# Two attention blocks with split queries: stacked halves for the scores, aggregated moments, and another order of slots

## The reference, cut to what matters

```
x = x + attention(ln(x), ctx, mask)    # X: 16 heads of 32, keys masked
x = x + ternary_ffn(quantised ln(x))   # one 512 x 512 product, rows quantised to 8 bits
x = x + attention(ln(x), ctx)          # Y: 16 heads of 64, with an output projection
x = x + ffn(ln(x))                     # Z: FFT, sparse product, inverse FFT, real part; folded into one matrix m
```

## Time and profile before

| | |
|---|---|
| median of 3 runs | 1170.33 us (1170.12 to 1173.37) |
| the profiled execution | 1169.09 us, its span 1167.3 us |
| PE busy | 957.4 us, 82% |
| DVE busy | 898.2 us, 77% |
| ACT busy | 634.9 us, 54% |
| POOL busy | 492.7 us, 42% |
| granted TensorE clock, mean | 0.91 |
| DMA moved | 131.95 MB, 113 GB/s |
| period of an item in the steady part | 110 us |

### The profile page before, as it was taken

The page is one execution under the profiler, slowest core; times in us unless marked ns, Lnnn a source line. Parts: engine busy times, 40 slices in busy tenths (PEclk is TensorE's granted clock), DMA queues, the critical chain, the costliest instruction groups (busy, mean ns, idle before and its releaser), DMA issues.

```text
span 1167.3 us, 17877 instructions
## 1 busy us (share of the span) xinstructions
PE 957.4 (82%) x6211; PEld 508.7 (44%) x6227; DVE 898.2 (77%) x1704; ACT 634.9 (54%) x1748; POOL 492.7 (42%) x437
## 2 busy tenths in 40 slices
PE   1896994693777997898799889979997898599694
PEld 0443463352343554454454445544554455344341
DVE  8777379537989799979987998899789978835732
ACT  2333174233577658657763776477558656614701
POOL 0224024111646267337723762475267336802603
PEclk9988997895699998999899989989998999699797
DMA  9623025543846747585648656746856483551612
GB/s 368 195 86 108 1 67 137 121 116 74 144 88 105 134 84 128 96 167 110 116 102 146 100 107 122 147 89 120 141 110 123 90 143 69 111 103 25 118 39 72
DMA packets 379026, 131.95 MB, mean 113 GB/s; under 512 B 365148, under 2 KB 370812, under 8 KB 375609
## 3 DMA queue, kind: packets, MB, share of 16 engines
q1 hardware_dynamic: 378937, 130.82, 54.7%
HBM read 35.14 MB, written 15.96 MB: 44 GB/s over the span
## 4 chain that ended last, share of the span: by engine, by line
DVE 35%; PE 24%; DMA 10%; ACT 9%; POOL 8%; SPq 8%; issue 7%; ACTq 0%; POOLq 0%; DVEq 0%
PE wb L170 6%; PE wb L171 6%; PE wb L172 6%; DMA prT<-ph 6%; DVE ph L1180 4%; ACT pr L770 3%; DVE mx L1158 3%; SPq L494 3%; PE wb L1307 2%; DVE xr L1112 2%; DVE stats L1052 2%; POOL xr L666 2%; DVE xn L1083 2%; DVE parts L862 2%; ACT xn L800 2%
## 5 line engine op out<-in xcount | busy, mean ns | idle before, releaser
L644 POOL TENSOR_TENSOR pr<-pr,sm 128x616 f32<-128x616 f32 x128 | 166.1, 1298 | 289.9 <-DVE sm L1175 283.0
L770 ACT ACTIVATE pr<-scores,mx,factor 128x77 f32<-128x77 f32 x576 | 229.6, 425 | 21.6 <-DVE mx L1161 18.4
L170 PE MATMUL wb<-xT,wq_hl 128*128 128x512 f16 x384 | 150.8, 393 | 9.6 <-DVE qc L1105 4.2
L171 PE MATMUL wb<-xT,wq_hl 128*128 128x512 f16 x384 | 150.6, 392 | 0.0
L172 PE MATMUL wb<-xT,wq_hl 128*128 128x512 f16 x384 | 149.6, 390 | 0.0
L783 ACT ACTIVATE ph<-pr 128x618 f16<-128x618 f32 x128 | 93.5, 732 | 97.0 <-DMA prT<-ph 75.6
L635 POOL TENSOR_TENSOR rstd<-var,mhalf 128x2 f32<-128x2 f32 (+1 forms) x48 | 51.2, 1067 | 221.4 <-DVE var L1068 221.4
L770 ACT ACTIVATION_READ_ACCUMULATOR pr<-scores,mx,factor 128x1 f32 x576 | 123.9, 215 | 0.0
L1112 DVE SCALAR_TENSOR_TENSOR xr<-wb,factor,xr 128x512 f32<-128x512 f32 x72 | 53.3, 740 | 71.7 <-PE wb L172 71.7
L1158 DVE TENSOR_REDUCE mx<-scores 128x8 f32<-128x616 f32 x128 | 101.1, 790 | 5.7 <-PE scores L172 5.6
L170 PE MATMUL scores<-k1b,qc 128*128 128x154 f16 x256 | 61.0, 256 | 49.3 <-DVE qc L1105 29.1
(11 more groups left out here) (218 smaller groups left out, 2502.6 us busy)
## 6 DMA issues: line engine op xcount, KB each, us to landing
xr<-in_x SPq DMA_DIRECT2D x6, 1024.0 KB, 6.1
out_x<-xr SPq DMA_DIRECT2D x6, 1024.0 KB, 5.2
prT<-in_dft SPq DMA_DIRECT2D x1, 3072.0 KB, 22.2
k1b<-scr_k SPq DMA_DIRECT2D x16, 154.0 KB, 6.8
scr_v<-k1b SPq DMA_DIRECT2D x9, 256.0 KB, 3.2
scr_k<-k1b SPq DMA_DIRECT2D x7, 308.0 KB, 3.1
xr<-in_wf SPq DMA_DIRECT2D x2, 1024.0 KB, 10.6
x<-in_x SPq DMA_DIRECT2D x2, 1024.0 KB, 10.7
```

The lines of the kernel that those rows point to most:

```text
L170: pe.matmul(out, lhs(0), rhs(0), start=start, stop=False, **kw)
L171: pe.matmul(out, lhs(0), rhs(1), start=False, stop=False, **kw)
L644: pool.tensor_tensor(v, v, s, ALU.mult).then_inc(probs_ready, 1)
L770: ins = act.activation(pr[U % 3][:, h // 4, cols], sc[:, U % 2, h // 4, cols], ACT.Exp, bias=mx[:, U % 4, h:h + 1], scale=k["factor"][:, f ...
```

## The change

1. **Stacked queries.** Each head pair's queries stand as one stack of 128 partitions: the 64 high rows in the lower half, their 64 low rows in the upper (`qc` and `q0T`, index 0 for the first two heads or first head, 1 for the other). K stands twice, once in either half (`load_k` issues each piece twice). A score is then two products, one with K's high and one with its low half, and contains low x low too. For X a group is the mask row and 4 matmuls of 154 columns, for Y 8 matmuls of 77 columns. ACT's and DVE's drains write where the halves already fit; what must cross partitions is moved by three DMAs of 64 x 512 per projection (`move_upper` once the high half is drained, `move_low` twice once the low half is). PE waits for these DMAs (`q0_stacked`, `q1_stacked`) where it waited for the drains. The low halves of Y's queries pass through `q0T`, so X's projections wait for their moves.
2. **Moments.** `ln_group` is one `bn_aggr` per tile; POOL adds the epsilon and negates the mean in two small operations more.
3. **Mask row.** It is kept in DRAM and loaded by SP; ACT's copy goes. The clear of `k1b` goes.
4. **Order.** New `FILLS` and `UNITS` (X in slots 0 to 4 and 6 to 8, nothing in 5 and 9), `HEADWISE` of 11 units in place of 9, `LOW_BY_POOL` of 2 in place of 6, other slots in `APPLY`, `LOWER`, `BIAS`; ACT and DVE take a unit's probabilities before the drains, not after.

```diff
-FILLS = [[("Z", "f", 0)],
-         [("Z", "f", 1)],
...
+FILLS = [[("Z", "f", 0), ("Z", "f", 1)],
+         [("Z", "f", 2), ("Z", "f", 3)],
+         [("Y", "pv", 4), ("Y", "pv", 5), ("Y", "pv", 6), ("Y", "pv", 7)],
          [],
+         [],
+         [("Z", "out", 0), ("Z", "out", 1), ("Z", "out", 2), ("X", "pv", 0)],
+         [("X", "pv", 1)],
+         [("Z", "out", 3), ("Y", "q", 0), ("Y", "q", 1)],
+         [("Y", "q", 2), ("Y", "q", 3)],
+         [("Y", "q", 4), ("Y", "q", 5)],
...
-HEADWISE = {("X", 0), ("X", 2), ("X", 5), ("X", 7), ("Y", 1), ("Y", 2), ("Y", 3), ("Y", 5), ("Y", 7)}
+HEADWISE = {("X", 0), ("X", 2), ("X", 5), ("X", 6), ("X", 7), ("Y", 1), ("Y", 2), ("Y", 3), ("Y", 4), ("Y", 6), ("Y", 7)}
-LOW_BY_POOL = {("X", 4), ("X", 6), ("X", 7), ("Y", 1), ("Y", 2), ("Y", 3)}
+LOW_BY_POOL = {("X", 7), ("Y", 1)}
...
                 for j in range(n):
                     rows = slice(j * w, (j + 1) * w)
-                    sp.dma_start(kb[rows, :, :, j, :].rearrange("p h m n -> p (h m) n"),
-                                 scr_k[rows, :, b * KEYS:(b + 1) * KEYS]).then_inc(kl, 16)
+                    for copy in range(2):
+                        r0 = copy * H1 + j * w % H1
+                        sp.dma_start(kb[r0:r0 + w, :, :, j, :].rearrange("p h m n -> p (h m) n"),
+                                     scr_k[rows, :, b * KEYS:(b + 1) * KEYS]).then_inc(kl, 16)
...
+            def move_upper(use):
...
+                sp.wait_ge(bank_hi, HIGH[use] + 1)
+                sp.dma_start(stack[0:H1, 1, m, :], stack[H1:P, 0, m, :]).then_inc(uppers_moved, 16)
+            def move_low(use, last):
+                stack, low, stacked = stack_of(use)
+                sp.wait_ge(bank_free, FILL[use] + 1)
+                sp.dma_start(stack[H1:P, 1, use[2], :], low[H1:P, :]).then_inc(stacked, 16)
+                sp.wait_ge(uppers_moved, 16 * (UPPER[last] + 1))
+                sp.dma_start(stack[H1:P, 0, use[2], :], low[0:H1, :]).then_inc(stacked, 16)
...
+                projected = [use for use in SLOT_DRAINS[g] if use[1] == "q"]
+                for use in projected:
+                    move_upper(use)
                 if unit_at(g - 2):
                     turn(*unit_at(g - 2))
+                for use in projected:
+                    move_low(use, projected[-1])
...
-                dve.tensor_tensor(m, e, o, ALU.add)
-                dve.tensor_tensor(h, e, o, ALU.subtract)
...
+                for t in range(t0, t0 + width):
+                    ins = dve.bn_aggr(moments[:, j, t, :], stats[:, j, t, :])
+                ins.then_inc(ln_var, 1)
...
-                if stage == "X" and u < 2:
-                    pe.wait_ge(bank_free, FILL["W", "q", 2 * u + 1, b] + 1)
+                if stage == "X" and u < 2:
+                    for m in (2 * u, 2 * u + 1):
+                        pe.wait_ge(q0_stacked[m], 32 * (b + 1))
...
+                        for e in range(4):
+                            for h in range(2):
+                                ins = pe.matmul(sc[:, U % 2, gg, e * KEYS:(e + 1) * KEYS], qc[:, e % 2, 2 * g + e // 2, tok],
+                                                k1b[:, h, 2 * g + e // 2, e % 2, :],
+                                                start=e == 0 and h == 0, stop=h == 1, skip_group_check=True)
```

154 lines of the change are left out of this document (79 added, 75 removed).

## The result

The changed kernel takes **1280.45 us** (median of four runs, 1278.3 to 1282.46), the kernel before 1171.01 us in the same comparison. The ratio is **1.092, 95% interval 1.090 to 1.095**: 109 us slower. The forecast was 1210 us with a range up to 1250. The sign is right, the size is not.

A forecast was written before the change was run, and what follows sets the result against it. DVE sets the pace in the item's first part, PE by a small margin in the second. Items of 104.6 + 5.7 + 6.4 + 2.6 = 119.3 us gave 49 more, less 9, on 1169.1: 1210 us, range 1132 to 1250.

The forecast's parts named there:

- Scores: PE's score matmuls in X and Y units: the new shapes save 3.9 us of PE per item.
- short matmuls cost as much: Rival, chance 0.02: short score matmuls cost as much as those of 154 columns, PE saves nothing there, 1225 us.
- Mean and variance: DVE's statistics groups: aggregations replace seven small operations, saving 0.5 us a group, 3 us an item.
- DVE in all: DVE's work per item, with statistics, exponentials, low halves and small scalings counted together: -2 us.
- SP (I): SP's queue in slot 4: transpose of X's unit 3 issues behind K and V loads, PE waits 5.7 us (3 to 8).
- SP (II): SP's queue, slots 8 and 9: K loads delay query moves, PE waits 6.4 us (4 to 9) before Y scores.
- The slots, the first part: From first Y scores to first output projection: 70.7 us becomes 64.6 (62 to 68).
- The second part: From first output projection to next Y scores: PE's own work is 40.0 us, with new waits and clock charge added.
- The start: Start-up of the kernel: saves about 5 us, as a clear of the keys goes.
- What I took off: On the whole time: 9 us taken off, as DVE, once it has waited, runs through its DVE-bound part faster.
- DMA engines become the bound: Rival, chance 0.08: DMA share becomes about 0.8, transposes land later, both waits grow 2 us or more, 1245 us.
- the waits stay hidden: Rival, chance 0.33: SP's issues overlap better or projections start later, 1131 us, or 1155 with a third of the waits.

## Why the prediction was right, and where it was wrong

The sign and both named places came out; the size did not, 1280.45 us where the forecast was 1210 and the range ended at 1250. The step that failed is the charge for the moves. It was made at one place in the item, ahead of unit 0 of Y, and at nothing in the first part and at the start, where PE and DVE wait for them as well. Of the 69 us between the sum and the trace, some 21 lie in the item's first part (3.5 in each of six items), 19 in its second, 19 at the start, and 9 are what was taken off. The steps follow one by one. (The bounds of the two waits, 8 and 9, give 1240 by the prediction's own sum, not its 1250.)

**The bound.** Right. The part that I called PE-bound by a small margin had 1.5 us of cover over one transpose, and moving that cover away is worth more than all that the change saves.

**Scores.** Right. The row is sixteen matmuls of 77 columns, and the next matmul starts 0.57 us behind their first:

```profile
733.79 0.73 PE L1311 MATMUL scores<-k1b,qc 128*128 128x77 f16 x16
734.36 0.38 PE L171 MATMUL wb<-xT,wq_hl 128*128 128x512 f16 x1
```

0.035 us each, as taken from the line between the rows of 64 and of 154 columns. The rival "short matmuls cost as much" is out. The Trainium skill's "TensorE: Matmul & The Clock Gate" (Wait — 56ns, not 53.3ns?) states a floor of some 62 ns a matmul with hardware decode off. It does not show here: sixteen at 62 ns would be 0.99 us. No run tells how decoding was set. An X unit takes 0.80 us where it took 1.05. That PE saves 3.9 us of work an item is so; that it saves that in time is not: some 2 us an item, even with the moves free.

**Mean and variance.** Right in kind, 3 us of DVE an item forecast, 3.4 measured. I let it act in the first part alone; by itself it takes 22 us off, the largest saving of the whole change that a run shows, and it hid behind the rest.

**DVE in all.** I took -2 us; it was -6.8 (95.9 to 89.1). The new tables alone gave -2.3, where my count of exponentials and low halves had given +1.1. It did not show in the time: DVE itself idled 11.1 us for the first scores, and where others waited for DVE (the quantised rows, the low buffer), DVE had waited before for PE or for moves.

**SP (I).** Right: a wait of 5.7 (3 to 8) forecast, 7.2 found; the issue 19.3 us after the output projection forecast, 20.9 found. The row transpose, four K pieces and V loads took 1.8, 5.6 and 6.95, where I had 2.0, 4.2 and 6.9. Its weight I had too small: taking it away saved 57 us, 9.5 us in each of six items on the mean, the 7.2 and the clock that a pause costs (0.91 granted in the item, not 0.88).

**SP (II).** Right, in part by luck: 6.4 (4 to 9) forecast, 8.2 to 8.6 found. The wait is the difference of two stretches from the end of the value product that ended wait (I), 800.1, and both were too short. The moves' way to the first scores took 31.2 us, not 27.9, and PE's work 23.0, not 21.5 (the granted clock was 0.81 from 799 to 809 us). DVE was on time (14.1 us for the 15 of the sum); SP then had a transpose and four moves of projections 0 and 1 ahead of the K pieces, which left at 18.3 us and not at 15.9. A move's issue is 0.59 to 0.6 us (a first one behind a transpose 0.9), where I took 0.43 from a plain small issue.

**The slots, the first part: a step that failed.** I had 64.6 us (62 to 68), found 68.1. Without the moves it is 61 to 64, so the term was good and what it left out is the moves' part: I costed those ahead of unit 0 of Y alone, and left the three places at nothing where DVE or PE wait for others (the low buffer, unit 4 of Y, the scores of X). The low buffer's 4.7 us is that, with 0.7 to 1.2 ahead of unit 4; a second buffer only moved 4.0 of it to the scores of X. Why the long wait ahead of unit 4 did not shrink, though DVE's drain is no longer the last there, is another thing: it moved to the exponentials, where I had ACT's room by its busy time alone. It has that room, in sum, and not between the scores of units 2 and 4.

**The second part** is 57.8 us, 54.7 by my sum (40.0 + 5.7 + 6.4 + 2.6). PE's own 40.0 is exact, as the run without moves shows; the waits are 3.3 larger in sum, and 2.4 are left for the clock. Together 6.6 us an item, in nearly every item.

**The start: a sign wrong.** I took -5 for the clear of the keys that goes; it is +13.7. Where no moves are, the first scores of Y begin at 316.8 us, 5.1 earlier than before; but with the new slots alone, which keep the clear, they begin at 313.4, so the gain is there and is not the clear's. With the moves, and eight K pieces between them, they begin 18.8 us later; 14.9 and 11.0 us of wait are left with the K pieces and the V pieces out of the way. The sum of the start held no SP term though the same three steps stand there.

**What I took off.** 9 us, as DVE would catch up after a wait. The seven periods show none of it. The 69 us between my sum (49 less 9, +40 against the profiled execution) and the trace (+109) are then: start 18.7, items 40, this 9, end 1.3.

**The rivals.** "DMA engines become the bound" did come near in time (1245) but for a reason that isn't so: their share in the item rose from 0.66 to 0.69, not to 0.8, and a transpose of probabilities lands in 3.7 us, 3.8 before. The queue issues late; the engines deliver as before. The runs with later loads reach 0.76 and 0.77 and are faster. That the waits stay hidden had 0.33 and no step of the trace for it.

## What to carry to other kernels

One in-order DMA queue is an engine like the others: count its steps an item, ask at every step who is behind it, and do so at all places where the change adds a wait, at the start too, not at the two that one looks at first. A halved matmul that needs its operand moved first buys fractions of a microsecond with a drain, an issue and one or two landings. If it must be, a slot of distance between the moves and their reader is what I would try; no run here has it. And when a change has many parts, time the smallest alone: here the aggregation was worth 22 us, so the other parts cost some 131, if the two add.

## What the runs showed that I had not expected

- Moving K pieces of 5 to 6 us of issue within a queue of that density gained 15 us in slot 14, nearly all of it at the start and the end, and 6 in slot 9, of 38 that the trace of the wait alone would give. Of the places tried, only the one where SP itself stands still (799.1 to 808.97) took loads without a wait coming back behind them.
- PE's part of an item came out at 40.0 us in each of four items once nothing in the queue stood in its way, to the tenth what the sum of starts had given. The parts that failed were nearly all waits.
- An issue of the same K pieces (four, 154 KB each) took 5.63 us in one place and 3.42 in the start, V pieces 6.95 and 6.49, where the first move of a group took 0.9 us or more and the next 0.6: what an issue costs depends on what stands before it in the queue, so I would now take the row at the same place, not the shortest.
- Seven small operations of DVE, 0.16 us each, stood in a group of statistics; two or four aggregations in their place took 22 us off 1171 over 48 groups, with 3.4 us of DVE's work and the clock's rise in each item.
- A move handed to another engine takes the conditions ahead of it along. ACT's 12 issues an item cost it 0.47 to 0.6 us each, and the landing it then had to wait for 6.2.
